# Half-array weights matmuls and column-strip joining matmuls in an edge-message kernel

## What is computed

```python
h_s = s @ lin1_ws * a ; h_v = einsum(v, lin1_wv) * a      # node table h, 12500 x 160
hid = silu(edge_scalars @ fc_w1)                          # per edge, 64 -> 64
w1, w2, w3, w4, w5 = split(hid @ fc_w2)                   # per edge, 64 -> 224
es, ev = h_s[edge_src], h_v[edge_src]                     # a gather of 160 floats per edge
mid_s = concat(w1*es*e0, w4*dot(ev, e1))                  # e0, e1: four numbers per edge
mid_v = concat((w2*es)*e1, w3*ev*e0, w5*cross(ev, e1))
agg_s, agg_v = segment_sum(mid_s, edge_dst), segment_sum(mid_v, edge_dst)
out = layernorm(x + gated(linear(x) + linear(agg)))
```

## Time and profile before

| | us |
|---|---|
| median of 3 runs | 4960.76 (4960.44 to 4968.37) |
| profiled execution, its own time | 4968.59 |
| its span, first to last instruction | 4966.8 |
| PE busy | 4335.4 (87%) |
| POOL busy | 2976.9 (60%) |
| DVE busy | 2456.7 (49%) |
| ACT busy | 1980.9 (40%) |
| mean granted TensorE clock | 0.970 of full |

### The profile page before, as it was taken

How to read it: one execution, slowest core, us unless ns; L and a number is a source line. 1 busy time by engine, 2 the same in 40 slices (tenths; PEclk the granted TensorE clock), 3 DMA queues, 4 the chain that set the end, 5 groups by cost and what they waited for, 6 DMA issues and landing times.

```text
span 4966.8 us, 71591 instructions
## 1 busy us (share of the span) xinstructions
PE 4335.4 (87%) x15455; PEld 1695.4 (34%) x15455; DVE 2456.7 (49%) x7618; ACT 1980.9 (40%) x5183; POOL 2976.9 (60%) x3139
## 2 busy tenths in 40 slices
PE   7888888888888888888888888888888888888887
PEld 6333333333333333333333333333333333333333
DVE  4444555554545454455444545444444444555454
ACT  2343434343434444444434443434343434343434
POOL 1666666666666666666666666666566666666663
PEclk9999999999999999999999999999999999999998
DMA  7333333333333333333333333333333333333333
GB/s 238 94 97 100 98 101 98 103 94 103 98 101 98 101 98 102 96 101 101 97 101 96 102 97 103 98 102 98 99 98 101 98 100 98 100 98 101 99 101 76
DMA packets 395154, 507.25 MB, mean 102 GB/s; under 512 B 71315, under 2 KB 277904, under 8 KB 394724
## 3 DMA queue, kind: packets, MB, share of 16 engines
q0 software_dynamic: 150144, 256.45, 20.4%
q1 hardware_dynamic: 172386, 133.82, 9.3%
q10 hardware_dynamic: 72578, 116.54, 8.1%
HBM read 426.47 MB, written 80.06 MB: 102 GB/s over the span
## 4 chain that ended last, share of the span: by engine, by line
another core or an unknown queue 39%; ACT 23%; issue 16%; PE 15%; SPq 2%; ACTq 1%; DMA 1%; DVE 0%; DVEq 0%
ACT aggsb L681 12%; ACT tsum L686 5%; PE psg L962 5%; PE psg L964 4%; PE pst_e L952 4%; ACT L707 2%; PE psw L943 1%; ACT hid L671 1%; PE psx L933 1%; SPq L549 1%; ACTq L664 1%; DMA agg_table<-aggsb 1%; PE psx L986 1%; SPq L557 0%
## 5 line engine op out<-in xcount | busy, mean ns | idle before, releaser
L637 POOL DMA_INDIRECT rows<-h_table,src_cols x3128 | 2975.4, 951 | 1943.3 <-issue 936.5
L523 DVE TENSOR_TENSOR prod<-psw,rows 128x384 f32<-128x384 f32 (+2 forms) x3128 | 1210.4, 449 | 1616.3 <-remote 863.0
L943 PE MATMUL psw<-fc,hid 128*128 128x480 f32 x3128 | 1473.5, 594 | 2.1 <-ACT hid L671 2.1
L681 ACT ACTIVATE aggsb<-psg 32x160 f32<-32x160 f32 x3128 | 919.2, 294 | 993.3 <-remote 450.8
L962 PE MATMUL psg<-tsum,shifts 128*128 128x448 f32 x1564 | 820.4, 608 | 333.8 <-ACT tsum L686 187.6
L943 PEld LDWEIGHTS psw<-fc,hid 128*128 128x128 f32 x3128 | 532.4, 190 | 926.3 <-issue 908.7
L952 PE MATMUL pst_e<-prod,sel 128*32 128x448 f32 x6256 | 768.2, 564 | 0.0
L964 PE MATMUL psg<-tsum,shifts 128*128 128x448 f32 x1562 | 764.9, 573 | 0.0
L933 PE MATMUL psx<-es,fc 128*128 128x512 f32 x782 | 428.6, 630 | 266.2 <-ACT turned L691 169.9
L686 ACT ACTIVATE tsum<-pst_e 128x448 f32<-128x448 f32 x782 | 425.6, 544 | 349.3 <-remote 210.0
L962 PEld LDWEIGHTS psg<-tsum,shifts 128*128 128x128 f32 x1564 | 246.0, 195 | 771.3 <-ACT tsum L686 364.9
(11 more groups left out here) (112 smaller groups left out, 1468.0 us busy)
## 6 DMA issues: line engine op xcount, KB each, us to landing
es<-in_esP ACTq DMA_DIRECT2D x391, 256.0 KB
agg_table<-aggsb SPq DMA_DIRECT2D x782, 80.0 KB
rows<-h_table,src_cols POOLq DMA_INDIRECT x3128
nag<-agg_table SPq DMA_DIRECT2D x96, 320.0 KB
out<-yn SPq DMA_DIRECT2D x97, 80.0 KB
h_table<-hrow ACTq DMA_DIRECT2D x24, 320.0 KB, 3.1
nxr<-in_x SPq DMA_DIRECT2D x96, 80.0 KB
xa<-in_xT SPq DMA_DIRECT2D x24, 256.0 KB, 2.6
```

The source lines that it names most:

```text
L523: return nc.vector.tensor_tensor(out, w_part, ev, ALU.mult)
L637: nc.gpsimd.indirect_dma_start(out=rows[:, u * QT + j, :], out_offset=None, in_=m.h, in_offset=bass.IndirectOffsetOnAxis(ap=m.src[:, t:t + ...
L681: ins = nc.scalar.activation(aggsb[r, b, :], picked(psg[r, :], k), ACT.Copy)
L943: ins = nc.tensor.matmul(both[:, 0:256 + WN], hid[:, at:at + P], m.fc2[:], start=True, stop=True)
```

## The change

The weights matmul no longer uses a block-diagonal matrix. `fc2` becomes [128, 224] with `fc_w2` on the upper and again on the lower 64 rows, and for each of the two column blocks of `hid` there are two matmuls, one that contracts rows 0 to 63 and one that contracts rows 64 to 127, with 224 columns each. The two write to different PSUM banks; which tile lies on which half of `hid` is altered to match in the host's layout `esP` and in the fallback program, which these inputs don't take. The clearing of `fc2` in the set-up goes.

The joining matmul is split into four column strips: strip k takes 32 stationary columns and only its own 160 moving columns, and writes them to columns 0 to 159 of its 32 PSUM partitions. So one ACT copy of 128 partitions by 160 elements takes the place of four. Semaphores, waits, their order and the gathers are the same.

```diff
--- before.py
+++ after.py
@@ -182,7 +182,7 @@
             r = slice(S * half, S * half + S)
             at = 0
             for src, width in W_ORDER:
-                late.append((m.fc2[r, 256 * half + at:256 * half + at + width], io["fc_w2"][:, src:src + width]))
+                late.append((m.fc2[r, at:at + width], io["fc_w2"][:, src:src + width]))
                 at += width
             late.append((m.fc1[r, r], io["fc_w1"]))
         n_w = 16 * (len(loads) + len(late))
@@ -253,7 +253,6 @@
                 c = slice(V * (i % 2), V * (i % 2) + V)
                 last = nc.vector.tensor_scalar(lw1z[r, c], l1v[r, :], V ** -0.5, None, ALU.mult)
             last.then_inc(s_lw, 1)
-            nc.vector.memset(m.fc2[:], 0.0)
             nc.vector.memset(m.fc1[:], 0.0).then_inc(s_fc, 1)
             dve.wait_ge(s_iota, 7)
             then(nc.vector.tensor_copy(iotf[:], iot[:]))
@@ -604,8 +603,8 @@
                     if not first:
                         sp.wait_ge(g_added, 16 * (QT * q + u))
                         sp.sem_inc(loads_seen, 1)
-                    h = S * (u % 2)
-                    sp.dma_start(es[0:S, 0:P], io["esP"][h:h + S, ds(q * CH + P * (u // 2), P)]).then_inc(g_es, 16)
+                    h = S * (u // 2)
+                    sp.dma_start(es[0:S, 0:P], io["esP"][h:h + S, ds(q * CH + P * (u % 2), P)]).then_inc(g_es, 16)
                     sp.dma_start(dstrow[:], io["dst"][ds(QT * q + u, 1), :].to_broadcast([P, P])).then_inc(g_dst, 16)
 
                 for u in range(QT):
@@ -676,10 +675,7 @@
                 act.wait_ge(quad_summed, q + 1)
                 if free:
                     act.wait_ge(agg_stored[b], 16 * i)
-                for k in range(K4):
-                    r = slice(W * k, W * k + W)
-                    ins = nc.scalar.activation(aggsb[r, b, :], picked(psg[r, :], k), ACT.Copy)
-                ins.then_inc(agg_copied, 1)
+                nc.scalar.activation(aggsb[:, b, :], psg[:, 0:AW], ACT.Copy).then_inc(agg_copied, 1)
 
             def copy_tiles(q, b):
                 act.wait_ge(tiles_summed, q + 1)
@@ -938,9 +934,11 @@
                 if free:
                     pe.wait_ge(prod_ready, 2 * r + b - 1)
                 for c in range(2):
-                    both = psw[b][:, 2 * c:2 * c + 2, :].rearrange("p t w -> p (t w)")
                     at = CH * b + P * c
-                    ins = nc.tensor.matmul(both[:, 0:256 + WN], hid[:, at:at + P], m.fc2[:], start=True, stop=True)
+                    for half in range(2):
+                        r = slice(S * half, S * half + S)
+                        ins = nc.tensor.matmul(psw[b][:, 2 * half + c, 0:WN], hid[r, at:at + P], m.fc2[r, :],
+                                               start=True, stop=True)
                 ins.then_inc(w_ready, 1)
 
             def sum_tiles(q, b, first):
@@ -959,9 +957,12 @@
                 pe.wait_ge(shifts_ready, q + 1)
                 if before:
                     pe.wait_ge(agg_copied, q)
-                ins = nc.tensor.matmul(psg[:, 0:PW], shifts[:, b, 0, :, :], tsum[:, b, :], start=True, stop=not before)
-                if before:
-                    ins = nc.tensor.matmul(psg[:, 0:PW], shifts[:, b, 1, :, :], tsum[:, 1 - b, :], start=False, stop=True)
+                for part in range(2 if before else 1):
+                    for k in range(K4):
+                        ins = nc.tensor.matmul(psg[W * k:W * k + W, 0:AW], shifts[:, b, part, k, :],
+                                               picked(tsum[:, b if part == 0 else 1 - b, :], k), start=(part == 0),
+                                               stop=(part == 1 or not before), tile_position=(0, W * k),
+                                               skip_group_check=True)
                 ins.then_inc(quad_summed, 1)
 
             def node_turn(k, width, bufs, c, landed):
@@ -1078,7 +1079,7 @@
         m.shift = sb("shift", [P, K4, W])
         m.spare = sb("spare", [P, 1], I32)
         m.fc1 = sb("fc1", [P, P])
-        m.fc2 = sb("fc2", [P, 256 + WN])
+        m.fc2 = sb("fc2", [P, WN])
         m.mscs = sb("mscs", [S, SO])
         m.mscv = sb("mscv", [3 * V, 3 * V])
         m.w5 = sb("w5", [P, CHUNKS, 2 * SO])
@@ -1108,7 +1109,7 @@
         "srcT": src.reshape(TILES, P).T, "dstT": dst.reshape(TILES, P).T, "dst": dst.reshape(TILES, P),
         "tile_base": dst.reshape(TILES, P)[:, 0:1].T,
         "e4T": e4.reshape(TILES, P, K4).transpose(1, 0, 2),
-        "esP": es.reshape(QUADS, 2, 2, P, S).transpose(2, 4, 0, 1, 3).reshape(2 * S, QUADS * CH),
+        "esP": es.reshape(QUADS, 2, 2, P, S).transpose(1, 4, 0, 2, 3).reshape(2 * S, QUADS * CH),
         "node_vec": node_vec1, "lin1_ws": L0_gnn_lin1_ws, "lin1_wv": L0_gnn_lin1_wv, "fc_w1": L0_gnn_fc_w1,
         "fc_w2": L0_gnn_fc_w2, "sc_ws": L0_gnn_sc_ws, "sc_wv": L0_gnn_sc_wv, "lin2_ws": L0_gnn_lin2_ws,
         "lin2_wv": L0_gnn_lin2_wv,
```

## The result

The changed kernel takes 6128.39 us (median of 4 runs, 6127.96 to 6143.47); the kernel before, measured beside it, 4964.57 us (median of 4, 4960.44 to 4976.75). The ratio is 1.2347 with an interval of 1.2317 to 1.2377: slower by 23%, far outside the range. Later measurements met a second condition of the chip, in which both kernels take about 4093 us; the experiments begin with it.

The account below looks back on a forecast made before the run. POOL's gather groups, each with one wait, were taken as the bound: 4968.6 - 78 (shorter waits) - 4 (after the last gather) = 4887 us, with the median 7.8 us lower, so 4880 us; range 4560 to 5040, likeliest case 4800 to 4950.

Parts of the forecast that it names:

- What bounds the kernel: POOL's groups of eight gathers plus one 2.59 us wait each, 12.3 us per group, set the time; PE's work does not.
- 391 x 12.3: Number of groups times group length with its wait, given as 4815 us from first to last gather.
- The parts' prices: Per quad at full clock: weights 1.71 to 0.9 us, joining 1.70 to 0.75, ACT's copy out 1.2 to 0.37.
- the 0.1 for the changed shape of the array: Joining on PE: 0.1 us added to 0.64 us for four waves, making 0.75 us.
- rival (e): Weights on PE: array halves don't run side by side; PE keeps 0.8 us per quad, forecast sum unchanged; no chance given.
- The order of signals and the second sums' end: Second sums end 5.9 us after restart, not 9.4; with PE's other signals gone ahead, POOL's wait shrinks slightly.
- The "0.2 us" of gain in the sum: POOL's wait per group shortens by 0.2 us, the middle between nothing and 0.38: 78 us in all.
- (b): Signal passes early, groups pair without a drain, later signals wait: +100 to +146 us, 5060 to 5107; chance 0.14.
- (c): Idle PE falls to half clock, second sums end over 12 us after restart: 5060 to 5150 us; chance 0.09.
- (a): Second sums' signal gets through midway, POOL skips its wait: down to 4070 us, 4660 with a third of groups; chance 0.22.
- (d): Nothing moves, within 0.2%: the signals' lateness follows the group's last gather alone; chance 0.13.

Follow-up runs that it names:

- the model: Late signals imitated where the kernel before takes 4093 us, by added waits for gathered rows: change with two waits 6063.99 us, with 14 filler matmuls too 5630.61 us.
- the relaxed wait: Changed kernel with POOL's wait ahead of gathers relaxed from tiles_summed of q-2 to q-5: 4091.49 us (0.9997), again 4096.71 us (0.9988).
- both held: Changed kernel; POOL and ACT's copy of the first quad's sums also wait until the group's rows have landed: 6063.99 us (1.4812); kernel before likewise: 6817.42 us.
- POOL held: Kernel before; POOL also waits, ahead of each group, until the previous group's rows have landed: 5054.35 us (1.2346); changed kernel likewise, other condition: 6126.77 us.

## Why the prediction was wrong, and where it was right

**What bounds the kernel: right.** The groups of gathers and the pause behind each are the clock of it: the waits explain 1120 of 1164 us. PE was never the bound, at 87% or at 58%. (The product 391 x 12.3 is 4809, not 4815; the trace has 4818 from the first to the last gather. Nothing hangs on it.)

**The parts' prices: near.** At full clock the joining takes 0.57 us (0.75 predicted, of which no run shows the 0.1 for the changed shape of the array), the weights 0.96 (0.9), the copy 0.303 (0.37). The halves of the array do contract side by side: in the trace their matmuls start 7 ns apart. This is the rule of the Trainium skill, "TensorE: Matmul & The Clock Gate", Part 3, on distinct row groups, and the trace agrees; rival (e) is out. The advice of the Trainium skill, same page, closing table, against idle gaps between bursts is borne out too, by a clock of 0.755 and, in the model, 433 us where the gap lies in the chain.

**The order of signals and the second sums' end: the step that failed.** The prediction put the second sums 5.9 us after the restart, on a joining and sums that start as soon as their data is there. They ended at 15.2 us. For that the first sums' announcement had to pass midway, as it does before, and I never asked what lets it pass. I had seen that announcements come late while gathers are in flight, and counted the lateness as a property of the group's end alone. With the new joining in front, the one announcement that the second half of the group hangs on falls out of the group: the joining alone lost it in the held condition (5925 us). What goes with this is the number of matmuls that PE has issued, 27961 in the profile's count where there were 15455, 16 in a joining for 4; that this number is the cause is argued. The "0.2 us" of gain in the sum became a loss of 2.88 us per group.

**The rivals.** (b) was the right family: announcements that miss the gathers wait for their end. But it had the pairing of groups as its way and half a microsecond as its price. (c)'s condition, second sums over 12 us after the restart, was met, though half clock did not bring it about: it came second, as 433 of 1010 to 1083 us (6064 against 5054 and 4981) in the model. (a)'s time came in the prompt condition, for both kernels, and not by its reason, for there the kernel before has no late signals either: 4070 us was given as the floor of the gathers, 4093 was measured. There the change has no effect, within 0.2%, which is (d)'s forecast and again not its reason: nothing of PE is on the path. In the condition of its own profile the range missed by the failed step; 4093 us would have missed it as well, because I took that condition for the only one.

**What stays open.** What makes a condition held or prompt; by what mechanism gathers delay PE's announcements; the weights part alone and the relaxed wait in the held condition, which were not met. No version here beats the kernel before by more than 0.12% in either condition; the nearest are the change and the relaxed wait in the prompt one (0.9996, 0.9997 and 0.9988).

## What to carry to other kernels

When a trace shows that an engine's signals are seen microseconds late, find which single signal still comes in time and what stands before it, for a change to the work there can lose it, however much busy time it saves: here a joining of 16 short matmuls for 4 long ones did. Price such a split in instructions too, not in columns alone. And measure the kernel before afresh beside each variant: here it moved by 17% between measurements, which would have drowned or faked every effect below that.

## What the runs showed of the hardware

- TensorE's completion signals passed within 0.05 us in the prompt condition (995 of 1000 or more of those recorded, in the profiles of before and of the change). In the held one, with indirect gathers of POOL in flight, a third (before) and half (change) of them did; the others came up to 5.7 and 8.8 us late, and those still due came together some 2 us after the last gather's end. Of ACT's and DVE's 97% or more passed within 0.05 us. Many steps of SyncE that take 0.07 us in the prompt condition took about 0.7.
- The same kernel took 4093 or 4965 us by the condition alone, 17.6% less or 21% more, with a granted clock near 0.97 to 0.996 in both.
- In the held condition PE's own starts dragged after many instructions: eight matmuls over 3.4 us.
- From the last gather's end to the landing of its rows it is 1.6 (both held) to 1.9 us (POOL held), by the medians of the runs with holds.
- Four column strips of 160 columns, four waves of them, take 0.57 us at 2.4 GHz and 1.07 at 1.2; with all 128 rows in use, their weight loads (110 ns each at 2.4 GHz) ran while matmuls of other strips were running.
